# First attention: projections of high and low parts in three fp32r passes, weights split on GpSimd, a new order on all engines

## The chip, the core and the metric

The program runs on one core of one Trainium2 chip. The metric is the device time of one execution in microseconds. A core has five engines that run their own instruction streams in order and wait for each other through semaphores: TensorE (PE, with its weight loads as PEld), VectorE (DVE), ScalarE (ACT), GpSimd (POOL) and SyncE (SP), which only issues transfers here. SBUF is the working memory, PSUM the memory that matmuls write.

## The reference, cut to what matters

The program computes a whole network (two cross attentions, two self attentions, two feed-forward parts). The change lies in the first self attention: eight layers of linear attention with 16 heads of 64 channels over 64 sequences of 32 tokens, followed by a feed-forward net, with the layers' weights as inputs.

```python
def _feature_map(x):
    return jax.nn.elu(x) + 1.0
# per layer, B = 8 layers, H = 16, D = 128, K = 64, F = 512:
# Wq, Wk, Wv (B, H, D, K), Wo (B, H*K, D), W1 (B, D, F), W2 (B, F, D), biases, two layer norms
```

As the kernel computes it: q and k go through the feature map; k is summed over a sequence, and so is k x v (element by element); attention is q x sum(kv) / (q x sum(k)). Then `x1 = norm(x + gelu(out))`, `x = norm(x1 + gelu(down(gelu(up(x1)))))`.

## The kernel before

All of it lies in `l0_attention`. Channels lie on the 128 partitions, the 2048 tokens along the free axis. The tokens are two halves of 1024. One **window** v is one half of one layer: 16 windows, v = 0 to 15. A window holds eight **units** u (two heads each, 128 channels). Unit n = 8v + u goes through these steps:

- TensorE: `project` (L251) three times, for q, k and v, each two matmuls of 512 columns in fp32 into PSUM `tile_q`, `tile_k`, `tile_v`. A profile shows one fp32 matmul as two records.
- ScalarE: `q_part` (L433, L434) and `k_part` (L440, L441), an exp and a relu each; `invert_den` (L445, L447), a reciprocal by log and exp.
- VectorE: `clip_q` (L588), `feature_q` (L592), `feature_k` (L599), `sum_k` (L605), `product_kv` (L611), `sum_kv` (L617), `attend` (L624).
- GpSimd: `den` (L774) and `num` (L777), two multiplications of 1024 columns.

Buffers of a unit are double (`b = u % 2`), so unit n waits for the release of unit n - 2.

What follows the attention of a window, its **tail**, is done in the next window, between that one's units: `out` (L262; eight blocks of 128 channels, in four calls of two, into PSUM `tile_t`), a gelu (L452), `add_residual` (L630), `mean` (L270), `centre` (L635), `square` (L460), `var` (L276), `rsqrt` (L464, L466), `normalise` (L639, L642), then the feed-forward: `up` (L289), four hidden gelus (L472), `down` (L295), a gelu (L479), and the second norm by the same lines, which gives the half's new `x`. That `x` is what the window after needs for its projections, since it has the same half in the next layer. `up` borrows `tile_k` and `tile_q`, so the units' projections wait for the hidden gelus.

The order on each engine is written out by hand in a function `window` for each of them; `all_windows` runs window 0 without a tail, twelve in a loop, three more, and `tail_alone` for the last tail. TensorE's rule at the start of a window is: `out(0)`, then a wait for the new `x`, then the first projection. ScalarE's gelus need a table load, and `log_exp_again` (L456) loads the other table behind them. Names in the profile carry an `a_`; `a_ps` is any of the four PSUM tiles.

Of the kernel before, what the change touches and what calls it, by code (L numbers as in the profile page):

```python
# [6 lines left out]
P = 128  # L7
B, S, D = 64, 32, 128
TOK = B * S
# [22 lines left out]
C_BIAS = WCOLS  # L32

# [121 lines left out]
def l0_attention(nc, x_in, consts, layers_dram):  # L155
# [5 lines left out]
    with ExitStack() as ctx:  # L161
# [9 lines left out]
        w = sb("w", [P, 2, WCOLS + BCOLS])  # L171
# [12 lines left out]
        hid = sb("hid", [P, FCH, HALF])  # L184

        w_loaded = [sem("w_loaded0"), sem("w_loaded1")]

        def first_layers(sp):
            for par in range(2):
                sp.dma_start(w[:, par, :], layers_dram[par]).then_inc(w_loaded[par], 16)  # L190
# [6 lines left out]
        q_parts, k_parts = sem("q_parts"), sem("k_parts")  # L197
# [8 lines left out]
        rstd, normed, affine = sem("rstd"), sem("normed"), sem("affine")  # L206
        res_done = sem("res_done")
# [4 lines left out]
        def col(par, c, n=1):  # L212
            return w[:, par, c:c + n]

        def bias(par, c):
            return w[:, par, C_BIAS + c:C_BIAS + c + 1]

        def bank(ap, j):
            return ap[:, j * BANK:(j + 1) * BANK]

        def all_windows(eng, window, tail_alone):
# [10 lines left out]
            window(last + 2, 1, 1, True)  # L232
            tail_alone(last + 2, 1)

        with nc.Block() as block:
            @block.sync
            def _(sp):
                with sp.Fori(0, (LAYERS - 2) // 2) as pair:
                    for par in range(2):
                        wait_ahead(sp, affine, 8 * pair + 4 * par + 4)  # L240
                        sp.dma_start(w[:, par, :], layers_dram[bass.ds(2 * pair + (par + 2), 1)].rearrange("a p c -> (a p) c")).then_inc(w_loaded[par], 16)

            @block.tensor
            def _(pe):
                def project(n, par, half, u, part):
                    tile, free, ready = ((tile_q, q_parts, q_ready), (tile_k, k_feat, k_ready),
                                         (tile_v, kv_prod, v_ready))[part]
                    wait_past(pe, free, n)
                    for j in range(2):
                        t0 = half * HALF + j * BANK  # L250
                        last = nc.tensor.matmul(bank(tile, j), col(par, part * HK + u * P, P),  # L251
                                                x[:, t0:t0 + BANK], start=True, stop=True)
# [26 lines left out]
                def ffn_up(v, par, n, c):  # L279
# [4 lines left out]
                    elif c < 3:  # L284
                        pe.wait_ge((k_feat, q_parts)[c - 1], n + 1)
# [6 lines left out]
                def ffn_down(v, par, j):  # L292
                    pe.wait_ge(hid_gelu, 4 * v + 4)
                    for c in range(FCH):
                        last = nc.tensor.matmul(bank(tile_t, j), col(par, C_W2 + c * D, D),  # L295
                                                bank(hid[:, c, :], j), start=(c == 0), stop=(c == FCH - 1))
# [3 lines left out]
                def window(v, par, half, tail):  # L300
                    tv, tp, th = v - 1, par if half else 1 - par, 1 - half

                    def q_of(u):
                        project(8 * v + u, par, half, u, 0)

                    def k_of(u):
                        project(8 * v + u, par, half, u, 1)

                    def v_of(u):
                        project(8 * v + u, par, half, u, 2)  # L310
# [5 lines left out]
                    def up(c):  # L316
                        if tail:
                            ffn_up(tv, tp, 8 * v + 4, c)

                    def down(j):  # L320
                        if tail:
                            ffn_down(tv, tp, j)
# [42 lines left out]
                    v_of(5)
                    q_of(6)
                    norm(mean, 1)
                    v_of(6)
                    k_of(7)
                    norm(var, 1)  # L370
# [3 lines left out]
                def tail_alone(v, par):  # L374
# [20 lines left out]
                    def down_part(j):  # L395
                        for c in range(FCH):
                            pe.wait_ge(hid_gelu, 4 * v + 4 * j + c + 1)
                            last = nc.tensor.matmul(bank(tile_t, j), col(par, C_W2 + c * D, D), bank(hid[:, c, :], j),
# [29 lines left out]
            def _(act):  # L428
                def q_part(n, par, u):
                    b = u % 2  # L430
                    wait_past(act, n_ready, n - 1)
                    act.wait_ge(q_ready, n + 1)
                    nc.scalar.activation(eq[:, b, :], tile_q[:, :], ACT.Exp, bias=bias(par, C_BQ + u))  # L433
# [15 lines left out]
                def gelu_out(v, par):  # L449
                    wait_ahead(act, normed, 2 * v)  # L450
                    wait_ahead(act, wo_done, v + 1)
                    nc.scalar.activation(g[:, :], tile_t[:, :], ACT.Gelu_apprx_tanh, bias=bias(par, C_BO)).then_inc(gelu_done, 1)  # L452
# [15 lines left out]
                def gelu_hidden(v, par):  # L468
                    wait_ahead(act, w2_done, v)
                    for c, tile in enumerate(UP_TILES):  # L470
                        act.wait_ge(hid_ready, 4 * v + c + 1)
                        nc.scalar.activation(hid[:, c, :], tile[:, :], ACT.Gelu_apprx_tanh,  # L472
# [9 lines left out]
                def window(v, par, half, tail):  # L482
                    tv, tp = v - 1, par if half else 1 - par
# [14 lines left out]

                    q_of(0)
                    k_of(0)  # L500
                    inverse(-1)
                    k_of(1)
                    q_of(1)
                    inverse(0)
                    k_of(2)
                    of_tail(gelu_out, tv, tp)
                    q_of(2)
                    inverse(1)
# [4 lines left out]
                    k_of(4)  # L513
                    q_of(4)
                    inverse(2)
                    of_tail(gelu_hidden, tv, tp)
                    k_of(5)
                    inverse(3)
                    q_of(5)
                    of_tail(gelu_down, tv, tp)  # L520
                    k_of(6)
                    inverse(4)
                    q_of(6)
                    of_tail(square, 2 * tv + 1)
                    k_of(7)
                    of_tail(rsqrt, 2 * tv + 1)
                    q_of(7)
                    inverse(5)
                    inverse(6)

                def tail_alone(v, par):
# [37 lines left out]
                    wait_ahead(act, w2_done, v)  # L569
# [11 lines left out]
                log_exp_again()  # L581
# [2950 lines left out]
```

## Time and profile before

| | |
|---|---|
| median of 3 runs | 2660.99 us (2655.34 to 2661.57) |
| the profiled execution | 2657.94 us |
| its span, first to last instruction | 2656.1 us |
| busy in the span: PE / DVE / ACT / POOL | 2419.6 / 2144.5 / 1883.3 / 791.4 us |
| mean granted TensorE clock | 0.963 of full |

The first attention takes the stretch from about 650 to 1957 us. Busy time of an engine is the time in which at least one of its instructions ran.

### The profile page before, as it was taken

The page shows a single profiled execution, that of the slowest core. Times are in us where ns is not written, and L with a number is a line of the kernel's source. Part 1 is how long each engine was busy: PE and PEld are TensorE (multiplying, and loading weights), DVE is VectorE, ACT ScalarE, POOL GpSimd, SP SyncE. Part 2 cuts the span into 40 slices and gives each one's busy share as a digit, 9 for nine tenths or more (in the row PEclk, how much of TensorE's full clock was granted, in tenths as well). Part 3 has the DMA queues.
Part 4 walks back from the last instruction along what each step waited for, and adds up shares of the span by engine and source line. Part 5 has one row for each costly group of instructions (what it writes and reads, how often), then busy time and mean ns, then how long its engine had stood idle before and what let it go on. Part 6 is the DMA issues. An engine that isn't in the chain of part 4 may idle for free. (4 is left out here: it accounts for less than half of the span.)

```text
span 2656.1 us, 29174 instructions
## 1 busy us (share of the span) xinstructions
PE 2419.6 (91%) x9257; PEld 1357.0 (51%) x9278; DVE 2144.5 (81%) x2857; ACT 1883.3 (71%) x2673; POOL 791.4 (30%) x466
## 2 busy tenths in 40 slices
PE   7899999998799999999999999999866899757998
PEld 3467776663344444444444444444323677444776
DVE  5787878872899999999999999999857888486454
ACT  6565555654789888998988898888756777435444
POOL 0121121111444444444444444444300000000554
PEclk9999999999899999999999999999986999977999
DMA  2000000002000101001010100100000011310211
GB/s 73 13 21 17 17 20 17 17 1 87 2 0 0 40 1 40 0 0 40 0 40 0 40 0 0 40 0 0 0 12 23 32 40 39 98 41 16 77 65 48
DMA packets 40927, 67.74 MB, mean 26 GB/s; under 512 B 15128, under 2 KB 31832, under 8 KB 39640
## 3 DMA queue, kind: packets, MB, share of 16 engines
q1 hardware_dynamic: 40512, 64.13, 7.4%
q10 hardware_dynamic: 288, 2.10, 0.2%
q8 instruction: 58, 0.95, 0.1%
q14 instruction: 69, 0.57, 0.1%
HBM read 60.91 MB, written 5.31 MB: 25 GB/s over the span
## 5 line engine op out<-in xcount | busy, mean ns | idle before, releaser
L251 PE MATMUL a_ps<-a_x,a_w 128*128 128x512 f32 x1536 | 695.4, 598 | 25.9 <-DVE a_kf L599 13.4
L251 PEld LDWEIGHTS a_ps<-a_x,a_w 128*128 128x128 f32 x1536 | 291.6, 191 | 405.1 <-issue 367.8
L774 POOL TENSOR_TENSOR a_den<-a_qf,a_ksum 128x1024 f32<-128x1024 f32 x128 | 271.0, 2117 | 512.0 <-DVE a_qf L592 475.3
L777 POOL TENSOR_TENSOR a_num<-a_qf,a_kvsum 128x1024 f32<-128x1024 f32 x128 | 294.8, 2303 | 185.5 <-DVE a_kvsum L617 185.5
L2705 ACT ACTIVATE x_sqk<-x_b_k 128x512 f32<-128x512 f32 x256 | 152.9, 597 | 149.1 <-PE x_b_k L2617 142.7
L2781 DVE TENSOR_REDUCE x_rn<-x_sqk 128x8 f32<-128x512 f32 x256 | 174.1, 681 | 91.7 <-ACT x_sqk L2705 87.4
L262 PE MATMUL a_ps<-a_att,a_w 128*128 128x512 f32 x480 | 215.8, 592 | 0.0
L592 DVE SCALAR_TENSOR_TENSOR a_qf<-a_eq,a_qf 128x1024 f32<-128x1024 f32 x128 | 195.2, 1525 | 1.7
L445 ACT ACTIVATE a_den<-a_den,consts 128x1024 f32<-128x1024 f32 x128 | 147.0, 1149 | 55.4 <-POOL a_den L774 55.4
L2598 POOL TENSOR_TENSOR x_kn<-x_craw,x_w 128x256 f32<-128x256 f32 x64 | 47.0, 734 | 464.5 <-DVE x_craw L2770 442.9
L599 DVE SCALAR_TENSOR_TENSOR a_kf<-a_ek,a_ps 128x1024 f32<-128x1024 f32 x128 | 155.4, 1214 | 29.6 <-ACT a_ps L441 24.7
L611 DVE SCALAR_TENSOR_TENSOR a_ek<-a_ps,a_w,a_kf 128x1024 f32<-128x1024 f32 x128 | 163.2, 1275 | 10.2 <-PE a_ps L251 10.1
L440 ACT ACTIVATE a_ek<-a_ps,a_w 128x1024 f32<-128x1024 f32 x128 | 142.1, 1110 | 37.3 <-PE a_ps L251 31.1
L2617 PE MATMUL x_b_k<-x_wk_hi,x_kt_hi 128*128 128x512 f32 x256 | 156.7, 612 | 4.7 <-DVE x_kt_lo L2776 4.7
L624 DVE SCALAR_TENSOR_TENSOR a_att<-a_num,a_den 128x1024 f32<-128x1024 f32 x128 | 155.6, 1216 | 5.3 <-ACT a_den L447 4.3
L433 ACT ACTIVATE a_eq<-a_ps,a_w 128x1024 f32<-128x1024 f32 x128 | 142.0, 1110 | 24.1 <-PE a_ps L251 15.5
L605 DVE TENSOR_REDUCE a_ksum<-a_kf 128x32 f32<-128x1024 f32 x128 | 155.1, 1211 | 1.1
L617 DVE TENSOR_REDUCE a_kvsum<-a_ek 128x32 f32<-128x1024 f32 x128 | 155.0, 1211 | 0.5
L1437 POOL TENSOR_TENSOR m_hid_lo<-m_hid,m_hid_hi 128x1024 fp32r<-128x1024 f32 (+1 forms) x43 | 102.7, 2402 | 173.8 <-ACT m_hid_hi L1393 173.8
L262 PEld LDWEIGHTS a_ps<-a_att,a_w 128*128 128x128 f32 x480 | 91.2, 190 | 114.8 <-issue 114.8
L434 ACT ACTIVATE a_qf<-a_ps,a_w 128x1024 f32<-128x1024 f32 x128 | 142.3, 1112 | 0.0
L441 ACT ACTIVATE a_ps<-a_ps,a_w 128x1024 f32<-128x1024 f32 x128 | 138.6, 1082 | 0.0
(423 smaller groups left out, 5189.1 us busy)
## 6 DMA issues: line engine op xcount, KB each, us to landing
a_w<-layers SPq DMA_DIRECT2D x8, 2577.0 KB, 9.7
x_craw<-ctx SPq DMA_DIRECT2D x32, 256.0 KB, 2.7
y_cx<-ctx_t SPq DMA_DIRECT2D x16, 512.0 KB, 3.7
m_wb<-m_scratch SPq DMA_DIRECT2D x16, 512.0 KB, 3.8
n_w<-experts SPq DMA_DIRECT2D x8, 544.0 KB, 5.0
x_w<-xattn_w ACTq DMA_DIRECT2D x1, 1536.0 KB, 9.4
x_all<-x_t SPq DMA_DIRECT2D x4, 256.0 KB, 9.4
t_scratch<-t_q_t SPq DMA_DIRECT2D x4, 256.0 KB, 3.5
```

The lines of the kernel that those rows point to most:

```text
L251: last = nc.tensor.matmul(bank(tile, j), col(par, part * HK + u * P, P), x[:, t0:t0 + BANK], start=True, stop=True)
L262: last = nc.tensor.matmul(bank(tile_t, j), col(par, C_WO + c * D, D), bank(att[:, half, c, :], j), start=(c == 0), stop=(c == CH - 1))
L592: nc.vector.scalar_tensor_tensor(out=qf[:, b, :], in0=eq[:, b, :], scalar=1.0, in1=qf[:, b, :], op0=ALU.add, op1=ALU.add).then_inc(q_feat, 1)
L599: nc.vector.scalar_tensor_tensor(out=kf[:, b, :], in0=ek[:, b, :], scalar=1.0, in1=tile_k[:, :], op0=ALU.min, op1=ALU.add).then_inc(k_feat, 1)
L605: nc.vector.tensor_reduce(ksum[:, b, :], by_batch(kf[:, b, :]), AX_X, ALU.add).then_inc(k_summed, 1)
L611: nc.vector.scalar_tensor_tensor(out=ek[:, b, :], in0=tile_v[:, :], scalar=bias(par, C_BV + u), in1=kf[:, b, :], op0=ALU.add, op1=ALU.mult ...
L617: nc.vector.tensor_reduce(kvsum[:, b, :], by_batch(ek[:, b, :]), AX_X, ALU.add).then_inc(kv_summed, 1)
L624: nc.vector.scalar_tensor_tensor(out=att[:, half, c, :], in0=num[:, b, :], scalar=1.0, in1=den[:, b, :], op0=ALU.mult, op1=ALU.mult).then_ ...
L774: nc.gpsimd.tensor_tensor(by_batch(den[:, b, :]), by_batch(qf[:, b, :]), bcast(ksum[:, b, :], S), ALU.mult).then_inc(d_ready, 1)
L777: nc.gpsimd.tensor_tensor(by_batch(num[:, b, :]), by_batch(qf[:, b, :]), bcast(kvsum[:, b, :], S), ALU.mult).then_inc(n_ready, 1)
L2617: last = nc.tensor.matmul(b_k[n % 2][:, :], a[:, b % 4, t], k[:, f], start=(p == 0), stop=(p == 2))
L2781: nc.vector.tensor_reduce(rn[:, b % 4, 8 * c:8 * c + 8], sqk[:, n % 2, :].rearrange("p (h d) -> p h d", d=XDH), AX_X, ALU.add).then_inc(n_ ...
```

## The change

**Projections.** `x` and the weights of q, k and v are split into a high part (rounded to fp32r) and a low part (the rest, rounded to fp32r). `project` does three matmuls in place of one fp32 matmul: high x high, low `x`, low weights. The weights come unit by unit (128 x 384 each) into one buffer `w_raw`, 56 transfers on SyncE's queue; GpSimd splits them (`split_unit`) in the windows of the second half, the first layer's ahead of everything. The high part of a new `x` comes from VectorE (`high_of`), the low part from GpSimd (`low_x`, one subtraction of 1024 columns per window); a window's TensorE work now starts with a wait for it (`x_split`).

**Other edits.** The gelus behind `out` and `down` write back to PSUM, and `add_residual` reads it there. The hidden layer lies in the buffer of `att`. `clip_q` waits for the exp alone; the relu alone waits for the q buffer's release. `normalise` is two steps. The order on TensorE, VectorE, ScalarE and GpSimd is new; the last units of a window finish in the next one.

```diff
             def _(sp):
+                for layer in range(LAYERS - 1):
+                    for u in range(CH):
+                        sp.wait_ge(w_split, 8 * layer + u + 8)
+                        sp.dma_start(w_raw[:, :], layers_dram[layer + 1][:, u * UCOLS:(u + 1) * UCOLS]).then_inc(raw_loaded, 16)
...
+                    if not half:
+                        pe.wait_ge(w_split, 4 * v + (u + 1))
...
-                        last = nc.tensor.matmul(bank(tile, j), col(par, part * HK + u * P, P),
-                                                x[:, t0:t0 + BANK], start=True, stop=True)
+                        for p, (a, b) in enumerate(((w_hi, x_hi), (w_hi, x_lo), (w_lo, x_hi))):
+                            last = nc.tensor.matmul(bank(tile, j), a[:, u, c], b[:, t], start=(p == 0), stop=(p == 2))
...
-                    out(0)
                     if not half:
                         pe.wait_ge(w_loaded[par], 4 * v - 8 * par + 16)
-                    wait_ahead(pe, affine, 2 * v - 2)
+                    pe.wait_ge(x_split, v + 1)
+                    out(0)
+                    k_of(0)
                     q_of(0)
-                    k_of(0)
+                    v_of(0)
                     out(2)
...
                 def q_part(n, par, u):
-                    wait_past(act, n_ready, n - 1)
+                    wait_past(act, q_feat, n - 1)
+                    act.wait_ge(q_ready, n + 1)
+                    nc.scalar.activation(eq[:, b, :], tile_q[:, :], ACT.Exp, bias=bias(par, C_BQ + u)).then_inc(q_exp, 1)
+                    wait_past(act, d_ready, n - 1)
+                    wait_past(act, n_ready, n - 1)
                     nc.scalar.activation(qf[:, b, :], tile_q[:, :], ACT.Relu, bias=bias(par, C_BQ + u)).then_inc(q_parts, 1)
...
-                    wait_ahead(act, normed, 2 * v + 1)
                     wait_ahead(act, w2_done, v + 1)
-                    nc.scalar.activation(g[:, :], tile_t[:, :], ACT.Gelu_apprx_tanh, bias=bias(par, C_BF2)).then_inc(gelu_done, 1)
+                    nc.scalar.activation(tile_t[:, :], tile_t[:, :], ACT.Gelu_apprx_tanh, bias=bias(par, C_BF2)).then_inc(gelu_done, 1)
...
+                def high_of(half, scale, shift):
+                    nc.vector.tensor_scalar(x_hi[:, half * HALF:(half + 1) * HALF], z[:, :], scale, shift,
+                                            ALU.mult, ALU.add).then_inc(x_high, 1)
...
+                def split_unit(u, raw, done):
+                    nc.gpsimd.tensor_copy(w_hi[:, u, :], raw).then_inc(w_high, 1)
+                    pool.wait_ge(w_high, done + 1)
+                    nc.gpsimd.tensor_tensor(w_lo[:, u, :], raw, w_hi[:, u, :], ALU.subtract).then_inc(w_split, 1)
...
+                            pool.wait_ge(x_high, v)
+                            nc.gpsimd.tensor_tensor(x_lo[:, t], x[:, t], x_hi[:, t], ALU.subtract).then_inc(x_split, 1)
...
+                for u in range(CH):
+                    split_unit(u, first_raw[:, u * UCOLS:(u + 1) * UCOLS], u)
```

ScalarE's order in the new window, by the names of the source: k0, inverse of the unit before last, q0, k1, inverse of the last, q1, k2, gelu behind `out`, inverse 0, q2, square, k3, q3, rsqrt, k4, inverse 1, q4, hidden gelus, k5, inverse 2, q5, gelu behind `down`, k6, inverse 3, square, q6, rsqrt, k7, inverse 4, q7, inverse 5.

Three places of the order. First, TensorE at the start of the first window in the loop (`a_ps3` is `tile_t`, so L262 is `out(0)` and `out(2)`; `a_ps0` is q, `a_ps1` k). Before:

```order
L262 MATMUL a_ps3<-a_att,a_w 128x512 x4
L63 ISA
L56 REGISTER_ALU
L251 MATMUL a_ps0<-a_x,a_w 128x512 x2
L251 MATMUL a_ps1<-a_x,a_w 128x512 x2
L257 REGISTER_ALU
L262 MATMUL a_ps3<-a_att,a_w 128x512 x4
```

And in the changed kernel, where L282 is `out(0)`:

```order
L277 ISA
L65 ISA
L282 MATMUL a_ps3<-a_att,a_w 128x512 x4
L58 ISA
L272 MATMUL a_ps1<-a_x_hi,a_w_hi 128x512
L272 MATMUL a_ps1<-a_x_lo,a_w_hi 128x512
L272 MATMUL a_ps1<-a_x_hi,a_w_lo 128x512
```

The wait for the new `x` stood between L262 and L251 and now stands ahead of L282; k comes first in place of q.

Second, VectorE around the first norm of a tail, from unit 2's products on. Before, where L639 and L642 are `normalise` and L592 is `feature_q` of unit 2:

```order
L635 TENSOR_TENSOR a_z<-a_z,a_ps 128x1024
L611 SCALAR_TENSOR_TENSOR a_ek<-a_ps,a_w,a_kf 128x1024
L588 TENSOR_SCALAR a_eq<-a_eq 128x1024
L592 SCALAR_TENSOR_TENSOR a_qf<-a_eq,a_qf 128x1024
L596 REGISTER_ALU
L599 SCALAR_TENSOR_TENSOR a_kf<-a_ek,a_ps 128x1024
L617 TENSOR_REDUCE a_kvsum<-a_ek 128x32
L611 SCALAR_TENSOR_TENSOR a_ek<-a_ps,a_w,a_kf 128x1024
L639 SCALAR_TENSOR_TENSOR a_z<-a_z,a_g 128x1024
L63 REGISTER_ALU
L642 TENSOR_SCALAR a_x<-a_z,a_w 128x1024
```

And in the changed kernel, where L662 and L667 are the two steps of the norm and L615 is `feature_q` of unit 2:

```order
L622 SCALAR_TENSOR_TENSOR a_kf<-a_ek,a_ps 128x1024
L634 SCALAR_TENSOR_TENSOR a_ek<-a_ps,a_w,a_kf 128x1024
L647 SCALAR_TENSOR_TENSOR a_att<-a_num,a_den 128x1024
L662 SCALAR_TENSOR_TENSOR a_z<-a_z,a_g 128x1024
L610 TENSOR_SCALAR a_eq<-a_eq 128x1024
L65 REGISTER_ALU
L667 TENSOR_SCALAR a_x<-a_z,a_w 128x1024
L615 SCALAR_TENSOR_TENSOR a_qf<-a_eq,a_qf 128x1024
```

`feature_q` of unit 2 stood five instructions ahead of the norm and now stands behind it.

Third, GpSimd. Before, its loop over the units:

```order
L774 TENSOR_TENSOR a_den<-a_qf,a_ksum 128x1024
L777 TENSOR_TENSOR a_num<-a_qf,a_kvsum 128x1024
L771 REGISTER_ALU
```

And in the changed kernel, from `den` of unit 4 in a window with splits on (L893 is `low_x`; L860 and L862 are a split):

```order
L849 TENSOR_TENSOR a_den<-a_qf,a_ksum 128x1024
L856 TENSOR_TENSOR a_num<-a_qf,a_kvsum 128x1024
L849 TENSOR_TENSOR a_den<-a_qf,a_ksum 128x1024
L893 TENSOR_TENSOR a_x_lo<-a_x,a_x_hi 128x1024
L884 REGISTER_ALU
L885 REGISTER_ALU
L860 CAST a_w_hi<-a_w_raw 128x384
L861 REGISTER_ALU
L862 TENSOR_TENSOR a_w_lo<-a_w_raw,a_w_hi 128x384
L849 TENSOR_TENSOR a_den<-a_qf,a_ksum 128x1024
```

Splits and the low part of `x` now stand between the multiplications.

## Rows read from the trace of the kernel before

**Rows 1.** Page, part 1: busy time in us, share of the span, instructions.

```profile
PE 2419.6 (91%) x9257; PEld 1357.0 (51%) x9278; DVE 2144.5 (81%) x2857; ACT 1883.3 (71%) x2673; POOL 791.4 (30%) x466
```

**Rows 2.** Windows view: stretch, length, busy of PE, PEld, DVE, ACT, POOL, clock.

```profile
700.00:1850.00 1150.00, 1114.32 (x2556) 480.88 (x2555) 1088.41 (x940) 1018.61 (x959) 521.24 (x237) 1.00 0.04 14
```

**Rows 3.** Timeline, PE: start us, length us, instructions; idle before in brackets.

```profile
725.35 3.60 PE L262 MATMUL a_ps<-a_att,a_w 128*128 128x512 f32 x8
...
1273.81 3.60 PE L262 MATMUL a_ps<-a_att,a_w 128*128 128x512 f32 x8
1277.86 3.69 PE L251 MATMUL a_ps<-a_x,a_w 128*128 128x512 f32 x8 [0.46 <-DVE a_x L642]
...
1348.49 3.60 PE L251 MATMUL a_ps<-a_x,a_w 128*128 128x512 f32 x8
1351.92 3.60 PE L262 MATMUL a_ps<-a_att,a_w 128*128 128x512 f32 x8
...
1903.16 12.27 PE L376 MATMUL a_ps<-a_att,a_w 128*128 128x512 f32 x28
```

**Rows 4.** Timeline, PE in the cross attention: the first and the fourth start.

```profile
305.34 0.39 PE L2617 MATMUL x_b_k<-x_wk_hi,x_kt_hi 128*128 128x512 f32 x1
...
306.03 1.89 PE L2652 MATMUL x_b_u<-x_yg,x_wvo 128*128 128x256 f32 x8
```

**Rows 5.** Timeline, DVE, one window.

```profile
1302.73 1.21 DVE L630 SCALAR_TENSOR_TENSOR a_z<-a_g,a_x 128x1024 f32<-128x1024 f32 x1
...
1306.12 1.21 DVE L635 TENSOR_TENSOR a_z<-a_z,a_ps 128x1024 f32<-128x1024 f32 x1
...
1315.90 0.81 DVE L642 TENSOR_SCALAR a_x<-a_z,a_w 128x1024 f32<-128x1024 f32 x1
...
1326.02 2.08 DVE L592 SCALAR_TENSOR_TENSOR a_qf<-a_eq,a_qf 128x1024 f32<-128x1024 f32 x1
...
1338.13 2.10 DVE L630 SCALAR_TENSOR_TENSOR a_z<-a_g,a_x 128x1024 f32<-128x1024 f32 x1 [0.75 <-ACT a_g L479]
...
1353.56 2.28 DVE L642 TENSOR_SCALAR a_x<-a_z,a_w 128x1024 f32<-128x1024 f32 x1
```

**Rows 6.** Timeline, ACT, the same window.

```profile
1300.48 1.11 ACT L452 ACTIVATE a_g<-a_ps,a_w 128x1024 f32<-128x1024 f32 x1
...
1320.87 1.28 ACT L472 ACT_TABLE_LOAD   x1
1322.16 4.30 ACT L472 ACTIVATE a_hid<-a_ps,a_w 128x1024 f32<-128x1024 f32 x4
...
1327.78 1.11 ACT L440 ACTIVATE a_ek<-a_ps,a_w 128x1024 f32<-128x1024 f32 x1
...
1329.79 1.15 ACT L445 ACTIVATE a_den<-a_den,consts 128x1024 f32<-128x1024 f32 x1
```

**Rows 7.** Timeline, POOL, the same window.

```profile
1325.10 1.91 POOL L774 TENSOR_TENSOR a_den<-a_qf,a_ksum 128x1024 f32<-128x1024 f32 x1 [10.32 <-DVE a_qf L592]
1326.97 2.89 POOL L777 TENSOR_TENSOR a_num<-a_qf,a_kvsum 128x1024 f32<-128x1024 f32 x1
```

**Rows 8.** Single lines, POOL: durations in ns, min/median/max, first and last start.

```profile
L774 POOL TENSOR_TENSOR a_den<-a_qf,a_ksum x128: 1902/1912/2892, 675.2 to 1914.7; 128x1024 f32<-128x1024 f32 x128
...
L1437 POOL TENSOR_TENSOR m_hid_lo<-m_hid,m_hid_hi x43: 2392/2397/2415, 2454.9 to 2640.1; 128x1024 fp32r<-128x1024 f32 x29, 96x1024 fp32r<-96x1024 f32 x14
...
L1749 POOL COPY t_qs<-t_q x8: 397/408/1317, 2316.9 to 2365.2; 128x256 f32<-128x256 f32 x8
```

**Rows 9.** Timeline, PE, first window of the attention.

```profile
676.24 3.70 PE L251 MATMUL a_ps<-a_x,a_w 128*128 128x512 f32 x8 [1.74 <-DVE a_kf L599]
683.14 8.83 PE L251 MATMUL a_ps<-a_x,a_w 128*128 128x512 f32 x16 [3.20 <-DVE a_ek L611]
```

**Rows 10.** Windows view, columns as in rows 2.

```profile
683.00:685.00 2.00, 1.86 (x3) 0.85 (x4) 1.97 (x3) 1.48 (x2) 0.89 (x1) 0.70 0.00 0
685.00:687.00 2.00, 2.00 (x4) 0.71 (x3) 2.00 (x3) 1.12 (x2) 0.00 (x0) 0.50 0.00 0
```

More of the change, by code:

```diff
@@ L170, in l0_attention @@
         x = sb("x", [P, TOK])
-        w = sb("w", [P, 2, WCOLS + BCOLS])
+        x_hi, x_lo = (sb(n, [P, TOK], F32R) for n in ("x_hi", "x_lo"))
+        w = sb("w", [P, 2, RCOLS])
+        w_raw = sb("w_raw", [P, UCOLS])
+        w_hi, w_lo = (sb(n, [P, CH, UCOLS], F32R) for n in ("w_hi", "w_lo"))
         att = sb("att", [P, 2, CH, HALF])
@@ L231, in all_windows @@
             window(last + 1, 1, 0, True)
-            window(last + 2, 1, 1, True)
+            window(last + 2, 1, 1, True, False)
             tail_alone(last + 2, 1)
@@ L581, in _ @@
                 log_exp_again()
+                for p in range(4):
+                    c = slice(p * BANK, (p + 1) * BANK)
+                    nc.scalar.activation(x_hi[:, c], x[:, c], ACT.Copy).then_inc(first_high, 1)
                 all_windows(act, window, tail_alone)
@@ L635, in centre, with normalise @@
                     nc.vector.tensor_tensor(z[:, part], z[:, part], tile_t[:, part], ALU.subtract).then_inc(z_centred, 1)
-                def normalise(k, out, scale, shift, part=slice(0, HALF)):
+                def normalise(k, part=slice(0, HALF)):
                     dve.wait_ge(rstd, k + 1)
@@ L640, in normalise, with scale_shift @@
                                                    op0=ALU.mult, op1=ALU.mult).then_inc(normed, 1)
+                def scale_shift(k, out, scale, shift, part=slice(0, HALF)):
                     wait_ahead(dve, normed, k + 1)
@@ L645, in x_of, with window @@
                     return x[:, half * HALF:(half + 1) * HALF]
-                def window(v, par, half, tail):
+                def high_of(half, scale, shift):
+                    nc.vector.tensor_scalar(x_hi[:, half * HALF:(half + 1) * HALF], z[:, :], scale, shift,
+                                            ALU.mult, ALU.add).then_inc(x_high, 1)
+                def window(v, par, half, tail, more=True):
                     tv, tp, th = v - 1, par if half else 1 - par, 1 - half
@@ L669, in attends, with features_q_of_last, sums_k_of_last, sums_kv_of_last @@
                         attend(8 * v + u, u % 2, half, u, v)
+                    def features_q_of_last(u):
+                        if tail:
+                            feature_q(8 * tv + u, u % 2)
+                    def sums_k_of_last(u):
+                        if tail:
+                            sum_k(8 * tv + u, u % 2)
+                    def sums_kv_of_last(u):
+                        if tail:
+                            sum_kv(8 * tv + u, u % 2)
+                    def attends_of_last(u):
+                        if tail:
+                            attend(8 * tv + u, u % 2, th, u, tv)
@@ new lines, in residual, with centres, normalised, affines @@
+                    def residual(i):
+                        if tail:
+                            add_residual(2 * tv + i, x1[:, :] if i else x_of(th), 2 * tv + i)
+                    def centres(i):
+                        if tail:
+                            centre(2 * tv + i)
+                    def normalised(i):
+                        if tail:
+                            normalise(2 * tv + i)
+                    def affines(i):
+                        if tail:
+                            scale_shift(2 * tv + i, x_of(th) if i else x1[:, :], bias(tp, C_S2 if i else C_S1), bias(tp, C_B2 if i else C_B1))
@@ L690, in window @@
[L690 to L692 removed]
+                    normalised(0)
                     clips_q(2)
+                    affines(0)
                     features_q(2)
[L695 to L699 removed]
                     features_k(4)
+                    sums_kv(3)
@@ L745, in x_part @@
                         return slice(HALF + j * BANK, HALF + (j + 1) * BANK)
-                    attend(8 * v + 7, 1, 1, CH - 1, v)
+                    sum_k(8 * v + 7, 1)
+                    sum_kv(8 * v + 7, 1)
+                    attend(8 * v + 5, 1, 1, 5, v)
+                    feature_q(8 * v + 7, 1)
+                    attend(8 * v + 6, 0, 1, 6, v)
+                    attend(8 * v + 7, 1, 1, 7, v)
                     for j in range(2):
@@ L765, in _ @@
                     dve.sem_inc(sem_ahead, 1)
+                for p in range(4):
+                    c = slice(p * BANK, (p + 1) * BANK)
+                    dve.wait_ge(first_high, p + 1)
+                    ins = nc.vector.tensor_tensor(x_lo[:, c], x[:, c], x_hi[:, c], ALU.subtract)
+                    if p % 2:
+                        ins.then_inc(x_split, 1)
                 all_windows(dve, window, tail_alone)
```

285 lines of the change are left out of this document (170 added, 115 removed).

## The prediction

> **What bounds the kernel now.** I read the page's busy shares first: TensorE 91%, VectorE 81%, ScalarE 71% of the span [rows 1]. The change touches only the first attention, so I asked for the busy time there: from 700 to 1850 us TensorE is busy 1114 of 1150 us, VectorE 1088, ScalarE 1019 [rows 2]. Three engines are nearly full, so what TensorE gives up is not simply won. TensorE's timeline gives the windows: the first `out(0)` starts at 725.35 and the lone tail at 1903.16, so the 15 windows with a tail take 1177.8 us, 78.5 each [rows 3]. A window holds 24 projections, four `out` calls, and norms and feed-forward worth 12 projections. Eight records start 3.43 us apart as a block (1348.49 to 1351.92), so a projection (four records) is 1.72 and an `out` 3.43. The sum is 24 x 1.72 + 4 x 3.43 + 12 x 1.72 = 75.6: TensorE waits only 3 us per window. One wait repeats: 0.46 us on `x` at 1277.86, just behind `out(0)` [rows 3].
>
> That wait matters. A window's tail must produce the `x` that the next window projects. So there is a loop: projections and `out` up to `out(6)`, gelu, norm, feed-forward, norm, `x`, and round again. Before, it is exactly as long as TensorE's work.
>
> **The change, part by part.** *Projections.* Three fp32r passes: the cross attention has such triples, and three passes take 305.34 to 306.03, 0.23 each [rows 4]. Six make 1.40 instead of 1.72: TensorE falls by 24 x 0.32 = 7.7 to 68 us per window. By the Trainium skill's page "FP8 and Floating Point Precision", section TensorE Precision Notes, true fp32 is four passes; three of them would be an estimated 1.29, and the loop below would be 0.8 shorter per window than by the row; measured, 1.40 is 0.82 of 1.72, not three quarters, so the row decides.
>
> *VectorE.* One instruction follows the next after 1.13 us (1302.73 to 1306.12 is three). I reckon 1.2 for a product and 0.6 for a clip, so a unit is 7.45 and eight are 59.6. The tail's eight were about 8.5, and the new `x_hi` adds one. So about 69 us of pure work. One `residual` took 2.10 and one `feature_q` 2.08 instead of 1.2 [rows 5]: GpSimd was in a multiplication from 1325.10, and GpSimd's next one took 2.89 [rows 7]. Instructions with two SBUF operands take turns with GpSimd. `residual` now reads PSUM, so its 0.9 goes.
>
> *GpSimd.* It gets `x_lo` every window, at 2.39 (the row of the same subtraction into fp32r), and eight splits in every second window. A split is a cast of 384 columns (0.41 for 256, so 0.6; up to 0.9 if writing fp32r costs what the subtraction costs) and a subtraction (2.39 x 384/1024 = 0.9) [rows 8]: 1.6, eight are 13.
>
> *ScalarE.* Same instructions: about 70 us of work. The gelu's table load can now run ahead of `down` (1.28 [rows 6]).
>
> **The loop after the change**, followed from the moment `x_split` lets TensorE start. Rates: VectorE as above, 1.25 until another engine sees the result; ScalarE two instructions in 2.01 (1327.78 to 1329.79), a reciprocal 2.2, the hidden gelus 1.28 + 4.30 [rows 6]; GpSimd 1.9 [rows 8]. Offsets of before are counted from `out(0)` at 1273.81.
> - `out(0)`, now behind the wait, and all up to `out(6)`: 4 x 3.43 + 7 x 1.40 = 23.5. Gelu starts at 23.7 (before 26.7 [rows 6]).
> - First residual 24.9 (28.9), VectorE's `feature_k(2)` and `sum_kv(1)`, `centre` 28.3 (32.3 [rows 5]): still 4 us gained.
> - ScalarE has the reciprocal of unit 0 and `q(2)` ahead of the square: 30.3. Variance 31.8 to 33.6. `k(3)` and `q(3)` stand ahead of the root: 35.3 to 37.5. `normalise` 37.6, clip, scale and shift 39.3 to 40.1 (before 42.1 to 42.9 [rows 5]).
> - Only now `feature_q(2)`, to 41.2. GpSimd then multiplies `num` and `den` of unit 2 to 45.1, and the relu of `q(4)` waits for both. It ends at 46.2, and the hidden gelus start there: 47.1 before [rows 6]. Three of the four us are gone.
> - Hidden gelus end 51.8; `q(5)` stands ahead of `down`: 53.2 to 60.1; gelu 60.5; second residual 61.7 (before 64.3 [rows 5]).
> - Two instructions of unit 5, `centre` 65.1; reciprocal of unit 3, square 67.4; variance to 70.2; `q(6)`, root to 72.6. Meanwhile GpSimd does `num` and `den` of unit 5 back to back until 72.5. The clip of unit 6 comes at 70.9 and must wait for it; `normalise` 74.3 instead of 72.6. Scale, shift and `x_hi` until 77.0 (before `x` was done at 82.0, from 1353.56 + 2.28 [rows 5]).
> - `x_lo` 2.4: 79.5, and the next window starts. Before, `out(0)` ran 3.43 us ahead of this point; now it stands behind it. So 5.0 us gained in the tail pay for 2.5 of `x_lo` and 3.5 of `out(0)`: 79.5 against 78.5.
>
> In windows with splits, `split(3)` stands between `num` and `den` of unit 2: 1.6 later from the hidden gelus on, 81.1.
>
> *The clock.* TensorE's last projection of the window ends at 74.4, so it sits idle for 5.1 us. In the first window it sat idle for 3.20 us before 683.14: the granted clock then was 0.70 and 0.50 (0.50 is 1.2 of 2.4 GHz), and 16 records took 8.83 us where 6.9 + 0.2 would do; after 1.74 us idle, 8 records took 3.70, which is full speed [rows 9, 10]. Five us resemble the first case: 1.9 us more, at the head of the loop. The price lies between 0 and 1.9; I take 1.9, by the nearest row. In windows with splits the wait for `q(4)` is 3.9 us: half a loss more, 0.5.
>
> **The sum.** 8 windows without splits at 81.4, 6 with at 83.5, the first one at 81.1 (it has VectorE's backlog and no idle stretch ahead of it): 1233, +55.5. The first window alone starts about 4 us later (eight splits and the split of `x` first), yet its projections and order let the next one start about 6 us earlier: -6. The end waits for no `x_lo`: -2 (0 to -4). Together +47. The profiled execution took 2657.94 us (span 2656.1), 3 below the median of the three runs. Forecast: 2705 us. If `x_hi` runs at the slow rate (1.2, as an instruction without the fast form, against the 0.81 of the `x` instruction), 6 us more; a cast at 0.9 shifts 7 windows by 0.3, 2 us more. My walk's error, 20 hand-overs of 0.1, is 2 us per window or 30 in all.
>
> **Rivals.**
> 1. *The loop shortens and VectorE binds: faster.* Its bare work is 23.5 + 46 = 69.5; my walk has 10 us of queueing. If that were 5, a window would be about 75, which VectorE's 69 plus the 5 us of turns with GpSimd also allow: 15 x (75 - 78.5) - 8 = -60, 2597 us. For it: seven of VectorE's instructions stand between `x_hi` and the next `feature_k(0)`, so that engine hardly idles there. Against: each queueing item above is an instruction that stands ahead in the new order. It decides below 78 us per window. Chance 0.21, spread from 2580 to 2650.
> 2. *The loop is as walked, but the clock holds:* 79.5 and 81.1, +26 - 8, 2676 us. For it: the page's clock in this stage is 1.00 [rows 2]. Against: no idle stretch there was long. Chance 0.16.
> 3. *GpSimd collides in every window with splits:* its 46 us and VectorE's 27 us of two-operand instructions must exclude each other, 73 of a window. If each split costs the tail one turn (4 us per such window), 2733 us. Against: most splits fall into GpSimd's pauses. Chance 0.13.
> 4. The forecast, 2685 to 2725 by its own: 0.50.
>
> **Chances and range.** About 0.3% (8 us) is what a measurement can tell from no change. Faster by more: 0.21. Within it: the lower part of rival 2, 0.07. Slower: 0.72. The range reaches down into rival 1 and up past rival 3: 2615 to 2750.
>
> **What would show it.** Right: TensorE idles about 5 us ahead of each `out(0)`, released by GpSimd's `x_lo`; the clock reads 0.5 just behind; `out(0)` starts come 80 to 84 us apart, longer where the splits are; projection records are 0.23 apart; the relu of `q(4)` waits for GpSimd. Wrong: `out(0)` starts under 78 us apart, or TensorE released there by something other than `x_lo`; then the queueing in my walk is the wrong step. If the starts are right and the clock reads 1.0, only the 1.9 is wrong.

## The result and the profile after

The changed kernel takes 2723.5 us in the median (2719.9 to 2727.8, four runs), the kernel before 2661.2. The ratio is 1.024 (95% interval 1.0218 to 1.0262): slower, by 62 us where 47 were forecast, inside the range. The profiled execution took 2719.86 us (span 2718.1).

Page, part 1 of the changed kernel (busy us, share of the span, instructions), and its windows view over 1120 us of the attention (stretch, length, busy of PE, PEld, DVE, ACT, POOL, clock):

```profile
PE 2355.6 (87%) x10025; PEld 1508.3 (55%) x10046; DVE 2115.1 (78%) x2876; ACT 1885.7 (69%) x2677; POOL 885.5 (33%) x609
...
760.00:1880.00 1120.00, 979.32 (x2995) 570.10 (x2994) 965.40 (x871) 938.12 (x884) 550.34 (x333) 0.95 0.05 16
```

In the attention the busy shares fell on all three big engines: 87%, 86% and 84%, where 97%, 95% and 89% stood before [rows 2]. No engine is full, and the mean clock fell to 0.95. That is the picture of a loop of waits. The timeline of PE shows it (start, length, instructions; in brackets the idle time before and who ended it; L272 projects, L282 is `out`, L309 `up`, L315 `down`, L290 `mean`):

```profile
722.19 3.59 PE L282 MATMUL a_ps<-a_att,a_w 128*128 128x512 f32 x8
...
1223.27 5.55 PE L282 MATMUL a_ps<-a_att,a_w 128*128 128x512 f32 x8 [5.35 <-POOL a_x_lo L893]
1228.26 0.79 PE L272 MATMUL a_ps<-a_x_hi,a_w_hi 128*128 128x512 f32 x1
1228.89 0.39 PE L272 MATMUL a_ps<-a_x_lo,a_w_hi 128*128 128x512 f32 x1
1229.12 0.40 PE L272 MATMUL a_ps<-a_x_hi,a_w_lo 128*128 128x512 f32 x1
...
1232.85 3.60 PE L282 MATMUL a_ps<-a_att,a_w 128*128 128x512 f32 x8
...
1273.19 1.98 PE L309 MATMUL a_ps<-a_x,a_w 128*128 128x512 f32 x4 [3.47 <-ACT a_qf L458]
...
1280.24 7.03 PE L315 MATMUL a_ps<-a_att,a_w 128*128 128x512 f32 x16
...
1290.04 1.98 PE L290 MATMUL a_ps<-a_z,consts 128*128 128x512 f32 x4
...
1306.88 6.41 PE L282 MATMUL a_ps<-a_att,a_w 128*128 128x512 f32 x8 [5.36 <-POOL a_x_lo L893]
1312.73 0.79 PE L272 MATMUL a_ps<-a_x_hi,a_w_hi 128*128 128x512 f32 x1
...
1317.32 3.60 PE L282 MATMUL a_ps<-a_att,a_w 128*128 128x512 f32 x8
...
1356.14 5.40 PE L309 MATMUL a_ps<-a_x,a_w 128*128 128x512 f32 x8 [1.95 <-ACT a_qf L458]
...
1390.91 5.36 PE L282 MATMUL a_ps<-a_att,a_w 128*128 128x512 f32 x8 [5.45 <-POOL a_x_lo L893]
...
1892.47 5.46 PE L282 MATMUL a_ps<-a_att,a_w 128*128 128x512 f32 x8 [5.20 <-POOL a_x_lo L893]
...
1969.06 9.08 PE L398 MATMUL a_ps<-a_att,a_w 128*128 128x512 f32 x20
```

Each of the 14 windows behind the first begins with some 5.35 us of idle time that GpSimd's `x_lo` ends. From the first `out(0)` at 722.19 to the lone tail at 1969.06 are 1246.9 us, where 1177.8 were before [rows 3]: +69.1. The 14 windows up to 1892.47 are 83.6 us each. The beginning came 3.2 us earlier, and what follows from the lone tail's start on is 3.9 us shorter (2718.1 - 1969.06 against 2656.1 - 1903.16). 69.1 - 3.2 - 3.9 = 62. The 3.9 us do not lie in the tail: it takes 53 us in both traces. They lie behind the attention, where the program is the same: from its last instruction to the end are 696.0 us against 700.5, and 696.7 to 699.9 in the traces of the experiments.

The windows view of the same execution shows the clock around 1306.88 (level 0.50 is 1.2 GHz):

```profile
1302.00:1304.00 2.00, 0.00 (x0) 0.00 (x0) 1.96 (x3) 1.97 (x3) 0.00 (x0) 1.00 0.01 4
1304.00:1306.00 2.00, 0.00 (x0) 0.00 (x0) 1.97 (x3) 2.00 (x3) 1.61 (x1) 0.89 0.00 0
1306.00:1308.00 2.00, 1.12 (x2) 0.60 (x3) 2.00 (x3) 1.82 (x2) 1.92 (x3) 0.50 0.00 0
...
1310.00:1312.00 2.00, 2.00 (x3) 0.67 (x2) 2.00 (x2) 0.00 (x0) 2.00 (x2) 0.50 0.37 98
1312.00:1314.00 2.00, 2.00 (x7) 1.23 (x6) 0.18 (x1) 0.00 (x0) 1.92 (x3) 0.91 0.00 0
```

The clock falls inside the idle stretch, and `out(0)` runs at half speed. The tail of the window, in the timelines of DVE, ACT and POOL:

```profile
1334.54 1.23 DVE L653 SCALAR_TENSOR_TENSOR a_z<-a_ps,a_x 128x1024 f32<-128x1024 f32 x1 [1.90 <-ACT a_ps L475]
...
1347.34 1.22 DVE L662 SCALAR_TENSOR_TENSOR a_z<-a_z,a_g 128x1024 f32<-128x1024 f32 x1
...
1382.00 2.28 DVE L610 TENSOR_SCALAR a_eq<-a_eq 128x1024 f32<-128x1024 f32 x1
...
1385.46 1.22 DVE L662 SCALAR_TENSOR_TENSOR a_z<-a_z,a_g 128x1024 f32<-128x1024 f32 x1
1386.71 0.81 DVE L667 TENSOR_SCALAR a_x<-a_z,a_w 128x1024 f32<-128x1024 f32 x1
1387.44 0.81 DVE L673 TENSOR_SCALAR a_x_hi<-a_z,a_w 128x1024 fp32r<-128x1024 f32 x1
```

```profile
1354.97 1.11 ACT L458 ACTIVATE a_qf<-a_ps,a_w 128x1024 f32<-128x1024 f32 x1 [2.70 <-POOL a_den L849]
1356.11 1.28 ACT L494 ACT_TABLE_LOAD   x1
```

```profile
1268.54 0.50 POOL L860 CAST a_w_hi<-a_w_raw 128x384 fp32r<-128x384 f32 x1
1269.12 1.00 POOL L862 TENSOR_TENSOR a_w_lo<-a_w_raw,a_w_hi 128x384 fp32r<-128x384 f32 x1
1270.08 1.91 POOL L849 TENSOR_TENSOR a_den<-a_qf,a_ksum 128x1024 f32<-128x1024 f32 x1
...
1353.03 1.91 POOL L849 TENSOR_TENSOR a_den<-a_qf,a_ksum 128x1024 f32<-128x1024 f32 x1
...
1381.81 1.92 POOL L849 TENSOR_TENSOR a_den<-a_qf,a_ksum 128x1024 f32<-128x1024 f32 x1
1388.32 2.36 POOL L893 TENSOR_TENSOR a_x_lo<-a_x,a_x_hi 128x1024 fp32r<-128x1024 f32 x1 [4.59 <-DVE a_x_hi L673]
```

### The profile page after: what moved, and what is told of

It is laid out like the page before. It is cut to its first block and busy times, and to the rows that moved or that the text cites. A ratio compares the mean times of both kernels' runs of the same rounds, so it can differ in the third digit from the quotient of the medians.

```text
span 2718.1 us, 31458 instructions
## 1 busy us (share of the span) xinstructions
PE 2355.6 (87%) x10025; PEld 1508.3 (55%) x10046; DVE 2115.1 (78%) x2876; ACT 1885.7 (69%) x2677; POOL 885.5 (33%) x609
## 5 line engine op out<-in xcount | busy, mean ns | idle before, releaser
L272 PE MATMUL a_ps<-a_x_hi,a_w_hi 128*128 128x512 f32 x768 | 370.8, 483 | 32.1 <-ACT a_qf L458 16.7
L856 POOL TENSOR_TENSOR a_num<-a_qf,a_kvsum 128x1024 f32<-128x1024 f32 x128 | 258.2, 2018 | 384.0 <-DVE a_qf L615 185.9
L282 PE MATMUL a_ps<-a_att,a_w 128*128 128x512 f32 x480 | 246.4, 661 | 75.1 <-POOL a_x_lo L893 69.5
L272 PE MATMUL a_ps<-a_x_hi,a_w_lo 128*128 128x512 f32 x768 | 307.0, 400 | 0.0
L272 PE MATMUL a_ps<-a_x_lo,a_w_hi 128*128 128x512 f32 x768 | 306.5, 399 | 0.0
L272 PEld LDWEIGHTS a_ps<-a_x_hi,a_w_hi 128*128 128x128 f32 x768 | 146.7, 191 | 112.9 <-issue 46.5
L282 PEld LDWEIGHTS a_ps<-a_att,a_w 128*128 128x128 f32 x480 | 100.9, 214 | 190.0 <-issue 173.5
L272 PEld LDWEIGHTS a_ps<-a_x_lo,a_w_hi 128*128 128x128 f32 x768 | 146.7, 191 | 62.3 <-issue 35.6
L309 PE MATMUL a_ps<-a_x,a_w 128*128 128x512 f32 x240 | 130.4, 674 | 55.8 <-ACT a_qf L458 39.9
L272 PEld LDWEIGHTS a_ps<-a_x_hi,a_w_lo 128*128 128x128 f32 x768 | 146.2, 190 | 35.2
L615 DVE SCALAR_TENSOR_TENSOR a_qf<-a_eq,a_qf 128x1024 f32<-128x1024 f32 x128 | 159.6, 1257 | 0.6
```

What stands on the lines that cost most here:

```text
L272: last = nc.tensor.matmul(bank(tile, j), a[:, u, c], b[:, t], start=(p == 0), stop=(p == 2))
L282: last = nc.tensor.matmul(bank(tile_t, j), col(par, C_WO + c * D, D), bank(att[:, half, c, :], j), start=(c == 0), stop=(c == CH - 1))
L615: nc.vector.scalar_tensor_tensor(out=qf[:, b, :], in0=eq[:, b, :], scalar=1.0, in1=qf[:, b, :], op0=ALU.add, op1=ALU.add).then_inc(q_feat, 1)
L856: nc.gpsimd.tensor_tensor(by_batch(num[:, b, :]), by_batch(qf[:, b, :]), bcast(kvsum[:, b, :], S), ALU.mult).then_inc(n_ready, 1)
```

## The experiments

All edits are to the changed kernel; the times are medians, and the ratios are to the kernel before. The theory is the loop as walked; the rivals are that VectorE binds, or that the clock costs nothing.

**1. `out(0)` ahead of the wait for `x`.**

```
+                    out(0)
                     if not half:
                         pe.wait_ge(w_loaded[par], ...)
                     pe.wait_ge(x_split, v + 1)
-                    out(0)
```

> TensorE issues out(0) ahead of its wait for the split of x; nothing else differs from the changed kernel. Theory (the loop as walked: x_lo releases the window, out(0) stands behind it): out(0) takes 3.04 us to the first projection and now fills part of the 5.35 us of idle time, so 2.3 us stay idle; the clock loss behind it (1.95 to 2.8 us at the head of each window now) shrinks to between 0 and 1.9. Each of 14 windows is 3.5 to 5.8 us shorter: 2643 to 2675 us, middle 2660. Rival (VectorE's 69 us of work and its turns with GpSimd bind the window; TensorE's place is only a symptom): within 10 us of the changed kernel's 2723.

2660.8 us, ratio to before 0.9999 (0.9987 to 1.0011). The timeline of PE, `out(0)` and what follows:

```profile
1285.19 3.59 PE L282 MATMUL a_ps<-a_att,a_w 128*128 128x512 f32 x8
1290.78 0.50 PE L272 MATMUL a_ps<-a_x_hi,a_w_hi 128*128 128x512 f32 x1 [2.00 <-POOL a_x_lo L893]
1291.12 0.39 PE L272 MATMUL a_ps<-a_x_lo,a_w_hi 128*128 128x512 f32 x1
1291.35 0.39 PE L272 MATMUL a_ps<-a_x_hi,a_w_lo 128*128 128x512 f32 x1
```

Within 1 us of the theory's middle: `out(0)` now runs in the idle time, 2.0 us of which stay, and in the window shown the projections behind it start 0.23 apart, at full clock. The edit takes away the whole loss against before, so VectorE did not bind. The 63 us are not `out(0)` alone, which is worth 14 x 3.0 = 43: the half clock goes from most window starts (in 5 of the 14 the three projections still take 5.8 in place of 4.3), but now strikes `up(2)` in all 15 windows, 20 us where it was 8. The trace is of the slowest of the ten executions, 2670.0 us.

**2. Four places for the relu of q.**

```
-        qf = sb("qf", [P, 2, HALF])
+        qf = sb("qf", [P, 4, HALF])
...
-                    wait_past(act, d_ready, n - 1)
-                    wait_past(act, n_ready, n - 1)
-                    nc.scalar.activation(qf[:, b, :], ...
+                    wait_past(act, d_ready, n - 3)
+                    wait_past(act, n_ready, n - 3)
+                    nc.scalar.activation(qf[:, u % 4, :], ...
...
```

`feature_q`, `den` and `num` take their place by `u % 4` too.

> The buffer qf for ScalarE's relu of q, two places now, has four, so relu of q(4) need not wait for GpSimd's num and den of unit 2; nothing else differs. Theory (the walk: that wait, 2.7 us in windows without splits and 4.2 with, puts off the hidden gelus and all that follows): each window about 3 to 4.2 us shorter, and in windows without splits the half clock at up(2) and up(3) goes too (1.2 to 1.5 us); together about 4 us by 15 windows, 2663 us (2655 to 2685). Rival (VectorE catches up with its backlog in the 4.8 us of idleness that stand behind that wait, and binds when they are gone): at most half of it, 2690 to 2723.

2670.6 us, ratio 1.0035 (1.0024 to 1.0047): 53 us less than the changed kernel. PE's timeline, `up(1)` to `up(3)` and the next `out(0)`:

```profile
1248.12 5.53 PE L309 MATMUL a_ps<-a_x,a_w 128*128 128x512 f32 x12 [0.28 <-DVE a_kf L623]
...
1284.60 5.95 PE L282 MATMUL a_ps<-a_att,a_w 128*128 128x512 f32 x8 [5.99 <-POOL a_x_lo L896]
```

The wait for `q(4)` is gone, three `up` run in a row, and windows are 80.2 us. A buffer of 8 KB more per partition was worth 3.5 us per window, the half clock at `up(2)` included (8 us in all).

**3. Work in the idle stretch.** `warm_head` issued ten throwaway products ahead of the wait, `warm_head5` five.

```
+                    if tail:
+                        pe.wait_ge(att_done, 8 * tv + 2)
+                        wait_ahead(pe, var_log, 2 * tv)
+                        for i in range(5):
+                            nc.tensor.matmul(bank(tile_t, i % 2), ..., start=True, stop=True)
                     pe.wait_ge(x_split, v + 1)
                     out(0)
```

> Ten throwaway products (4.3 us at full rate) fill most of TensorE's 5.35 us of idle time ahead of out(0); out(0) overwrites them, and the order and the waits are those of the changed kernel. Theory (the half clock behind the idle stretch costs 1.95 to 2.8 us per window at the head of the loop): out(0) takes 3.0 to the first projection in place of 5.0 to 5.9, each of 14 windows 2.0 to 2.8 shorter, 2685 to 2695 us; out(0) starts about 81.3 us apart. Rival 1 (the granted clock reads low but the loop does not feel it, something behind it waits anyway): 2715 to 2725. Rival 2 (the clock falls for another reason than idleness): still 0.5 behind out(0), 2723.

2747.8 us, slower by 24: my mistake of counting a float32 product as one record, so that the ten took 8.6 us and held `out(0)` back. It says nothing on what the clock costs.

> As warm_head, but five throwaway products: a float32 product is two records of 0.43 us, so warm_head's ten took 8.6 us and held out(0) back by 3; five take 4.3 us of the 5.35 us of idle time. Theory (half clock behind the idle stretch costs 1.95 to 2.8 us per window): out(2) starts 8.6 us behind out(0)'s release in place of 9.6 to 10.4; each of 14 windows up to 2 us shorter, 2690 to 2705 us, less where the half clock behind the wait of up(2) changes its windows. Rival (the loop does not feel the clock): 2718 to 2728.

2701.3 us, ratio 1.0149 (1.0132 to 1.0166), 22 less than the changed kernel. PE's timeline, `out(0)` and `out(2)` of one window and `up(2)` of two:

```profile
1266.94 6.43 PE L309 MATMUL a_ps<-a_x,a_w 128*128 128x512 f32 x8 [3.47 <-ACT a_qf L464]
...
1302.56 3.70 PE L282 MATMUL a_ps<-a_att,a_w 128*128 128x512 f32 x8 [0.97 <-POOL a_x_lo L899]
...
1310.29 3.60 PE L282 MATMUL a_ps<-a_att,a_w 128*128 128x512 f32 x8
...
1349.12 1.99 PE L309 MATMUL a_ps<-a_x,a_w 128*128 128x512 f32 x4 [1.95 <-ACT a_qf L464]
```

From `out(0)` to `out(2)` 7.73 us, against 9.58 and 10.44 above: the half clock cost 1.9 and 2.7 there. Windows are 80.2 without splits, where `up(2)` keeps full speed, and 83.7 with them, where it doesn't. Over all windows the starts give back 29 us and `up(2)` takes 7 more: the 22. The loop feels the clock. Rival 2 of the prediction falls.

**4. `x_lo` on VectorE**, right behind `x_hi`; GpSimd's `low_x` goes.

```
+                    dve.wait_ge(x_high, v)
+                    nc.vector.tensor_tensor(x_lo[:, t], x[:, t], x_hi[:, t], ALU.subtract).then_inc(x_split, 1)
```

> x_lo is computed by VectorE right behind x_hi instead of by GpSimd. Theory (x_lo's 2.36 us lie on the path from x_hi to out(0)): about 1.25 us plus a hand-over on VectorE in its place, each of 14 windows 0.9 to 1.3 us shorter, 2705 to 2711 us, TensorE's idle time ahead of out(0) 4.2 in place of 5.35. Rival (VectorE binds): its work per window grows by 1.2 us, 2735 to 2742.

2724.8 us, ratio 1.0237 (1.0220 to 1.0254): neither; the same as the changed kernel. Windows without splits are 81.2 us (1310.42 to 1391.65), those with splits 86.1 (1224.31 to 1310.42), where the changed kernel has 84.0 and 83.6 in these two places:

```profile
1274.85 6.50 PE L309 MATMUL a_ps<-a_x,a_w 128*128 128x512 f32 x8 [3.47 <-ACT a_qf L458]
...
1310.42 5.78 PE L282 MATMUL a_ps<-a_att,a_w 128*128 128x512 f32 x8 [5.15 <-DVE a_x_lo L679]
...
1359.05 1.98 PE L309 MATMUL a_ps<-a_x,a_w 128*128 128x512 f32 x4 [1.95 <-ACT a_qf L458]
...
1391.65 6.12 PE L282 MATMUL a_ps<-a_att,a_w 128*128 128x512 f32 x8 [4.25 <-DVE a_x_lo L679]
```

The idle time that ends the window without splits is 1.2 shorter, as expected (4.25 for 5.45); the other 1.6 us of its gain are less half clock, at its start and at `up(2)`. The one that ends the window with splits is only 0.2 shorter: GpSimd, free of `x_lo`, is at the next split already (from 1303.47 on), and VectorE's `normalise` takes 2.01 us beside it, from 1305.44 (1.22 above). And `up(2)` of that window now runs at half clock, after the same 3.47 us of idle time after which the changed kernel ran at full speed (1273.19). So the 1.2 us that `x_lo` costs on GpSimd show in every other window, and the sum hides them.

**5. A fourth pass in each projection**, which gives TensorE 11.2 us more per window.

```
-                        for p, (a, b) in enumerate(((w_hi, x_hi), (w_hi, x_lo), (w_lo, x_hi))):
+                        for p, (a, b) in enumerate(((w_hi, x_hi), (w_hi, x_lo), (w_lo, x_hi), (w_lo, x_lo))):
```

> Each projection gets a fourth pass (low part of the weights by low part of x), so TensorE works 24 x 0.47 = 11.2 us more per window, 180 us in all; order and waits are those of the changed kernel. Theory (TensorE is not what binds the window, only its 7 projections of the head lie on the loop): +3.3 us at the head, while the idle stretch ahead of out(0) shrinks by the others and the 2 to 2.8 us of half clock behind it go: 0 to +2 us per window, 2720 to 2755 us. Rival (TensorE's work sets the window as before): +5 us or more per window once the 5.35 us of idle time are used up, 2790 to 2900 us.

2827.5 us, ratio 1.0622 (1.0604 to 1.0640): +104, in the rival's range. My expectation falls, but not to the rival's reason: TensorE still idles 3.74 us ahead of `out(0)`.

```profile
1265.46 6.32 PE L282 MATMUL a_ps<-a_att,a_w 128*128 128x512 f32 x8 [3.74 <-POOL a_x_lo L893]
...
1320.66 5.54 PE L309 MATMUL a_ps<-a_x,a_w 128*128 128x512 f32 x8 [3.47 <-ACT a_qf L458]
1329.75 7.03 PE L315 MATMUL a_ps<-a_att,a_w 128*128 128x512 f32 x16
...
1340.34 1.88 PE L290 MATMUL a_ps<-a_z,consts 128*128 128x512 f32 x4
...
1357.11 6.57 PE L282 MATMUL a_ps<-a_att,a_w 128*128 128x512 f32 x8 [3.73 <-POOL a_x_lo L893]
```

From `out(0)` at 1265.46, `down` starts after 64.3 us and the second mean after 74.9; in the changed kernel it was 57.0 and 66.8 (`out(0)` at 1223.27). The tail's products stand in TensorE's one queue behind projections, so those projections lie on the loop too. From the first `out(0)` to the end of the attention the trace is 101 us longer, 6.7 per window. About 10 of the 101 are more half clock at the windows' starts: from `out(0)` to `out(2)` are 11.8 and 12.0 us in the two kinds of window, where the first one, with no idle time ahead, takes 9.0. The rest is 6.1 per window, about 13 projections' worth (0.47 each) of 24. By the same share, what three passes save is worth an estimated 13 x 0.32 = 4.2 us per window; no run measures that directly.

**6. Splits cut to one column** in the loop, so that layers after the first project with the first layer's weights.

```
+                    c = slice(0, UCOLS if isinstance(done, int) and done < CH else 1)
-                    nc.gpsimd.tensor_copy(w_hi[:, u, :], raw).then_inc(w_high, 1)
+                    nc.gpsimd.tensor_copy(w_hi[:, u, c], raw[:, c]).then_inc(w_high, 1)
```

> GpSimd's splits of the weights inside the loop are cut to one column of 384 (so layers after the first compute with the first layer's weights in the projections); order and waits are those of the changed kernel. Theory (a split costs the loop only where it stands between num and den of unit 2, 1.6 us in each of 7 windows, and a little at the first window): 10 to 15 us less, 2708 to 2715 us, give or take 15 us as the half clock behind the wait of up(2) may change its windows. Rival (splits collide with VectorE all over the window, 4 us or more in each of 7 windows on top of that): 40 us less or more, below 2685 us.

2701.4 us, ratio 1.0145 (1.0122 to 1.0167): 22 less, within the theory's margin, outside the rival's. The wait of `up(2)` is 2.33 in place of 3.47 us, 8 us by 7 windows. Nearly all of the rest is the clock's: half clock costs 6 us less at `up(2)` (from the third window on none runs it at half speed) and 6 less at the windows' starts. Windows with and without splits are 82.2 and 81.7.

**7. Both mended, and a version that beats both.** `out0_qf4` is 1 and 2 together; `out02_qf4` issues `out(2)` ahead of the wait as well (shown against `out0_qf4`):

```
                     out(0)
+                    out(2)
                     if not half:
...
                     v_of(0)
-                    out(2)
```

> out(0) ahead of the wait for the split of x, and four places for qf. Theory (the walk: both lie on one loop, one after the other, so their gains add): qf4's windows are 80.2 us; 3.04 less for out(0), and the 2 us behind the idle stretch, which shrinks to 2.6, go in part: 75 to 77.2 us per window, 2597 to 2629 us, middle 2612. Rival (VectorE's 69 us and its turns with GpSimd bind as soon as one of the two is mended): the gains don't add, 2640 to 2660.

2602.4 us, ratio 0.9782 (0.9765 to 0.9798): 2.2% faster than before, in the theory's range. Gains of 63 and 53 make 121 together, so they lie one behind the other.

> As out0_qf4, and out(2) ahead of the wait for the split of x too; the two take 6.1 us, as long as the idle stretch. Theory: no idle time at the head and no half clock behind it, 72.3 us by the walk; VectorE's 69 us with 5 us of turns then bind, 73 to 75 us per window: 2570 to 2598 us. Rival (the new order of VectorE holds the next thing back, the products of the last units of the window before, so that out(6) waits): no better than out0_qf4, 2597 to 2629.

2601.8 us, ratio 0.9777 (0.9761 to 0.9794): nothing more, in the rival's range and not in the theory's. In the windows view and in PE's timeline, `out02_qf4`:

```profile
760.00:1880.00 1120.00, 1043.67 (x3297) 610.45 (x3296) 1072.13 (x966) 1034.82 (x982) 604.26 (x357) 1.00 0.05 16
...
1413.36 0.50 PE L272 MATMUL a_ps<-a_x_hi,a_w_hi 128*128 128x512 f32 x1 [1.71 <-DVE a_kf L623]
...
1423.60 3.70 PE L282 MATMUL a_ps<-a_att,a_w 128*128 128x512 f32 x8 [0.53 <-DVE a_att L648]
```

`x_lo` ends no wait of TensorE any more; `k(1)` (1413.36) waits for VectorE's `feature_k` of unit 0, and `out(6)` (1423.60) for an `attend` of the window before. VectorE is busy 96% of the time, TensorE 93% at full clock. `out0_qf4` has 1068 us of VectorE in the same stretch. This fits VectorE as the bound, at about 75 us per window, where rival 1 of the prediction had it. Whether the amount of its work or the order of it sets the 75 is not shown; a run with less of VectorE's work was not made.

## Why the prediction was right, and where its sizes were off

- **The loop as walked.** Right. Counted from 1306.88, less the 2.7 us of half clock: residual 25.0 (forecast 24.9), `normalise` 37.8 (37.6), relu of `q(4)` begun 45.4 and ended 46.5 (46.2). The clip of unit 6 takes 2.28 us, as `den` holds GpSimd until 1383.73; second `normalise` 75.9 (74.3), `x_hi` done 78.7 (77.0). Of what the last two are late, 1.0 is the half clock at `up(2)`. By `warm_head5` a window without splits and without half clock is 80.2, against 79.5: the walk was 0.7 short, of the 2 that it allowed itself. By the Trainium skill's page "SBUF — State Buffer", section Who interferes with whom, a fast `tensor_scalar` and a GpSimd instruction block each other for the whole instruction; the clip's 2.28 us, which end 0.55 behind `den`, at 1384.28, agree.
- **`x_lo` and `out(0)` behind it pay for what the tail gained.** Right: 5.35 us idle (5.1 forecast), `x_lo` 2.36 (2.4), and experiment 1 gives back 63 us, the clock's part included.
- **`num` and `den` of unit 2 hold the relu.** Right: ended by `den` at 1354.94; experiment 2 gives back 53 us. With a split between them (0.50 + 1.00 and hand-overs) the wait of `up(2)` is 3.47 in place of 1.95: 1.5 us for the forecast 1.6.
- **The clock.** Right in kind, too small in size. From `out(0)` to `out(2)` the 14 windows lose 1.7 to 2.7 us, 2.1 in the mean. The forecast took 1.9 from [rows 9]; with the 0.2 that it names itself the row gives 8.83 - 7.1 = 1.7. At `up(2)` the forecast gave 0.5 to windows with splits alone; measured, `up(2)` to the next projection takes 3.85 us at full speed and up to 2.0 more, in windows of both kinds, 8 us in all for 3.
- **The sum.** Six windows with splits take 83.9 (83.5 forecast), seven without 83.2 (81.4), the first one 84.5 (81.1). Together these 14 are 18.4 us over the forecast: 10 by the walk's 0.7 in each, 5 by the clock at `up(2)`, 3 by the clock at their starts. The last window, which no `x_lo` ends, is 4.8 shorter than its 81.4, for the 2 that the forecast gave to the end. The first window won 3.2 for 6. The 3.9 us from behind the attention stood in no term; since that stretch takes 696.0 to 700.5 us in the traces of this case, they are luck of these two executions, and without them the profiled loss would have been 66.
- **What was to show it.** `x_lo` ends the idle time, the clock reads 0.5 behind it, projection records are 0.23 apart, the relu of `q(4)` waits for GpSimd: all as said. The starts lie 82.2 to 84.6 apart, but where the splits are only 0.7 longer in the mean, for 2.1 forecast: that part was wrong. The half clock costs more where no splits are, at the start 2.4 us against 1.8, and at `up(2)` it strikes windows of both kinds.
- **Rivals.** 1, VectorE binding at 75 us per window, did not happen in this order; what is left once the order's two waits are mended fits it, but it is not shown. 2 is refuted by experiment 3. 3, collisions of splits, by experiment 6: 22 us, of which 8 are the wait of `up(2)` and some 12 the clock.

## What to carry to other kernels

When an engine that was full is relieved, look for the longest loop from one stage to the next, and walk it instruction by instruction in the new order: here TensorE got 7.7 us less to do per window, and one product behind a wait instead of ahead of it (63 us in all, the clock's part included) and, in the new order, a buffer with two places where four were wanted (53 us) outweighed it. Work that needs nothing of what is waited for goes ahead of the wait. What a pass saves counts only for the passes ahead of something that is waited for: here, by experiment 5, those of some 13 of 24 projections.

## What the hardware showed that was not expected

- The same idle time does not always cost the clock. After 1.95 us ahead of `up(2)` TensorE ran at half speed at 1356.14 (granted clock 0.50 from 1357 to 1360) and at full speed in `warm_head5` at 1349.12 (1.00 throughout); after 3.47 us at full speed at 1273.19 (1.00) and at half speed in `xlo_dve` at 1274.85 (0.50 up to 1280). What else decides stays open; whole windows changed by 2 us with it, which nearly hid the price of `x_lo`.
- At full clock an fp32r pass of 512 columns starts 0.233 us after the last. Four passes over two banks, an estimated 8 x 0.233 = 1.87 us, are dearer than float32's 1.72 for the same [rows 3].
